# Inverse roots of two layer norms: pow on GpSimd, or Sqrt on ScalarE and a reciprocal on VectorE

## The reference

```python
def _layernorm(x, axis=-1, eps=1e-05):
    m = jnp.mean(x, axis=axis, keepdims=True)
    v = jnp.var(x, axis=axis, keepdims=True)
    return (x - m) / jnp.sqrt(v + eps)
...
x = x + jnp.tanh(g_xattn[0]) * _L0_xattn_ref(ctx_1024, _layernorm(x, axis=-1), ...)
x = x + jnp.tanh(g_ffn[0]) * _L0_ffn_ref(_layernorm(x, axis=-1), ...)
x = x + jnp.tanh(g_xattn[1]) * _L1_xattn_ref(_layernorm(x, axis=-1), ctx_1024, ...)
x = x + jnp.tanh(g_ffn[1]) * _L1_ffn_ref(_layernorm(x, axis=-1), ...)
```

## Time and profile before

| | |
|---|---|
| three runs | 1621.97, 1613.87, 1620.56 us; median 1620.56 |
| the profiled execution | 1621.97 us, of which the span of the profile is 1620.1 |
| busy share of the span | PE 91%, DVE 70%, ACT 60%, POOL 33% |
| mean granted clock of PE | 0.96 |
| attention block starts at | 873 us of the span |
| FFN block starts at | 1427 us of the span |

### The profile page before, as it was taken

The page is one execution under the profiler, slowest core; times in us unless marked ns, Lnnn a source line. Parts: engine busy times, 40 slices in busy tenths (PEclk is TensorE's granted clock), DMA queues, the critical chain, the costliest instruction groups (busy, mean ns, idle before and its releaser), DMA issues. The chain is left out here.

```text
span 1620.1 us, 21635 instructions
## 1 busy us (share of the span) xinstructions
PE 1466.9 (91%) x6308; PEld 640.0 (40%) x6309; DVE 1139.5 (70%) x1679; ACT 976.4 (60%) x1528; POOL 531.1 (33%) x342
## 2 busy tenths in 40 slices
PE   5678988889979899999999788899999999999899
PEld 2334434434434344444444343332333333244344
DVE  7989999999986222222223857789999999548975
ACT  3999999999933001111111542477878878868764
POOL 0679788688950710000003655605000000000000
PEclk7899989989989999999999899899999999999999
DMA  5202102002572565357524625354232332120344
GB/s 180 70 21 57 48 21 72 20 23 70 181 246 101 194 135 196 129 193 262 201 91 142 214 93 160 113 189 118 72 88 76 81 83 76 53 104 1 70 110 120
DMA packets 133478, 181.30 MB, mean 112 GB/s; under 512 B 46451, under 2 KB 80627, under 8 KB 132387
## 3 DMA queue, kind: packets, MB, share of 16 engines
q1 hardware_dynamic: 111878, 132.48, 27.7%
q0 software_dynamic: 6624, 23.14, 4.7%
q10 hardware_dynamic: 14912, 24.89, 4.6%
HBM read 109.29 MB, written 54.92 MB: 101 GB/s over the span
## 5 line engine op out<-in xcount | busy, mean ns | idle before, releaser
L265 POOL TENSOR_TENSOR m_hs<-m_hs,m_C 128x1024 f32<-128x1024 f32 x128 | 302.3, 2379 | 76.1 <-DVE m_hs L476 75.5
L1811 DVE TENSOR_REDUCE a_mx<-a_s 128x2 f32<-128x1024 f32 x256 | 303.2, 1218 | 33.1 <-PE a_s L1925 29.7
L476 DVE TENSOR_TENSOR_SCAN m_hs<-m_dA,m_d 128x512 f32<-128x512 f32 x256 | 293.7, 1200 | 9.4 <-PE m_d L622 8.5
L622 PE MATMUL m_d<-ident_sb,m_dBuT 128*128 128x128 f32 x1024 | 161.3, 289 | 30.8 <-DVE m_hs L476 23.2
L622 PEld LDWEIGHTS m_d<-ident_sb,m_dBuT 128*128 128x128 f32 x1024 | 115.7, 145 | 159.4 <-DVE m_hs L476 86.0
L371 ACT ACTIVATE m_dA<-m_dt,m_negA 128x512 f32<-128x512 f32 x256 | 168.1, 710 | 6.3 <-DVE m_hs L476 4.4
L1249 PE MATMUL e_gu<-e_w,e_xgT 128*128 x376 | 169.2, 592 | 0.0
L349 ACT ACTIVATE m_dBuT<-m_dtuT,m_BT 128x512 f32<-128x512 f32 x241 | 157.7, 710 | 0.1
L1925 PE MATMUL a_s<-ring_sb 96*128 96x512 bf16 x512 | 150.2, 383 | 4.5 <-DVE a_mx L1811 3.1
L917 ACT ACTIVATE e_sg<-e_gu 128x256 f32<-128x256 f32 x47 | 18.0, 384 | 224.6 <-PE e_gu L1249 224.6
L637 PE MATMUL m_y<-m_hs,m_fold 128*64 128x512 f32 x512 | 143.0, 639 | 0.4 <-POOL m_hs L265 0.4
(11 more groups left out here) (335 smaller groups left out, 2449.2 us busy)
## 6 DMA issues: line engine op xcount, KB each, us to landing
e_w<-in_ex_gu SPq DMA_DIRECT2D x16, 1024.0 KB, 6.2
ring_sb<-qk_dram SPq DMA_DIRECT2D x64, 192.0 KB, 3.1
xg_dram<-zeros_sb SPq DMA_DIRECT2D x2, 6016.0 KB, 28.3
e_xg<-xg_dram ACTq DMA_DIRECT2D x47, 256.0 KB, 2.7
yg_dram<-attn_sb ACTq DMA_DIRECT2D x47, 256.0 KB, 2.0
m_C<-c_dram SPq DMA_DIRECT2D x64, 128.0 KB, 2.9
m_dt<-m_dt SPq DMA_DIRECT2D x64, 128.0 KB, 2.3
e_w<-in_ex_dn SPq DMA_DIRECT2D x16, 512.0 KB, 7.5
```

The lines of the kernel that those rows point to most:

```text
L265: pool.tensor_tensor(hs[:, J % RH], hs[:, J % RH], C2[:, N % RC].unsqueeze(1).broadcast_to([P, 2, L]), ALU.mult).then_inc(s_hc, 1)
L476: dve.tensor_tensor_scan(hs[:, J % RH, h], dA[:, j % RA], pd[j % RD][:], 0.0, ALU.mult, ALU.add)\
L622: last = pe.transpose(pd[j % RD][:, t * P:(t + 1) * P], dBuT[:, N % 2, t, g], ident[:])
L1811: dve.tensor_reduce(mx[:, r % 2, h * TB + 2 * c:h * TB + 2 * c + 2], psc[c][:], AX.X, ALU.max)\
```

## The change

In both blocks the pow on POOL goes, with the `power` column it reads and its wait. ACT gets a function `std(b)`, a Sqrt in place on the four columns, and DVE's `inverse(b)` gets a reciprocal ahead of the `nmr` instruction. The new Sqrts stand on ACT after value 9 (batch 0), after value 15 (1), after `normalise(1)` (2) and after `normalise(2)` (3); in the FFN block ahead of each `normalise(b)` for batches 0 to 2, and that of batch 3 right after `normalise(2)`. `normalise(b)` waits as before for `inverse(b)`, whose semaphore now counts two steps for each batch.

```diff
@@ attention, gpsimd
-            def inverse_root(b):
-                cols = slice(b * TB, (b + 1) * TB)
-                pool.wait_ge(s_st, 2 * b + 2)
-                pool.tensor_tensor(rstd[:, cols], rstd[:, cols], power[:], ALU.pow).then_inc(s_rs, 1)
-
-            pool.memset(power[:], -0.5).then_inc(s_pw, 1)
-            pool.wait_ge(s_pw, 1)
...
-                if t in (8, 12):
-                    inverse_root(t // TB - 2)
-            inverse_root(2)
-            inverse_root(3)
@@ attention, scalar
+            def std(b):
+                act.wait_ge(s_st, 2 * b + 2)
+                cols = slice(b * TB, (b + 1) * TB)
+                act.activation(rstd[:, cols], rstd[:, cols], ACT.Sqrt).then_inc(s_sd, 1)
...
             def normalise(b):
-                act.wait_ge(s_inv, b + 1)
+                act.wait_ge(s_inv, 2 * b + 2)
...
             for t in range(10):
                 copy_v(t)
+            std(0)
             copy_v(10)
             copy_v(11)
             normalise(0)
             for t in range(12, NT):
                 copy_v(t)
+            std(1)
             normalise(1)
+            std(2)
             normalise(2)
+            std(3)
             act.preload_act_table_set("natural_log_exp_and_others")
@@ attention, vector
             def inverse(b):
                 cols = slice(b * TB, (b + 1) * TB)
-                dve.wait_ge(s_rs, b + 1)
+                dve.wait_ge(s_sd, b + 1)
+                dve.reciprocal(rstd[:, cols], rstd[:, cols]).then_inc(s_inv, 1)
+                dve.wait_ge(s_inv, 2 * b + 1)
                 dve.scalar_tensor_tensor(nmr[:, cols], mv[:, cols, 0], -1.0, rstd[:, cols], ALU.mult, ALU.mult)\
                     .then_inc(s_inv, 1)
@@ FFN, gpsimd
-            pool.memset(power[:], -0.5).then_inc(s_c, 1)
-            pool.wait_ge(s_c, 4)
-            for b in range(NT // TB):
-                cols = slice(b * TB, (b + 1) * TB)
-                pool.wait_ge(s_ln, SEQ * (b + 1))
-                pool.tensor_tensor(rstd[:, cols], rstd[:, cols], power[:], ALU.pow).then_inc(s_rs, 1)
@@ FFN, scalar
+            def std(b):
+                cols = slice(b * TB, (b + 1) * TB)
+                act.wait_ge(s_ln, SEQ * (b + 1))
+                act.activation(rstd[:, cols], rstd[:, cols], ACT.Sqrt).then_inc(s_lsd, 1)
+
             def normalise(b):
-                act.wait_ge(s_q, 2)
-                act.wait_ge(s_inv, b + 1)
+                act.wait_ge(s_inv, 2 * b + 2)
...
             round_weight(0)
+            std(0)
             normalise(0)
             square(1)
+            std(1)
             normalise(1)
             weight_std(1)
             round_weight(1)
             copy_x(0)
+            std(2)
             normalise(2)
+            std(3)
@@ FFN, vector
             def inverse(b):
                 cols = slice(b * TB, (b + 1) * TB)
-                dve.wait_ge(s_rs, b + 1)
+                dve.wait_ge(s_lsd, b + 1)
+                dve.reciprocal(rstd[:, cols], rstd[:, cols]).then_inc(s_inv, 1)
+                dve.wait_ge(s_inv, 2 * b + 1)
                 dve.scalar_tensor_tensor(nmr[:, cols], mv[:, cols, 0], -1.0, rstd[:, cols], ALU.mult, ALU.mult)\
                     .then_inc(s_inv, 1)
```

More of the change, by code:

```diff
@@ L1395, in attention @@
         rstd = sb("rstd", [P, NT])
-        power = sb("power", [P, TB])
         nmr = sb("nmr", [P, NT])
@@ L1436, in attention @@
         s_st = sem("ln_steps")
-        s_pw = sem("power_set")
-        s_rs = sem("ln_inverse_roots")
+        s_sd = sem("ln_std")
         s_inv = sem("ln_ready")
@@ L2102, in attention_out_and_ffn @@
         s_ln = sem("ln_steps")
-        s_rs = sem("ln_inverse_roots")
+        s_lsd = sem("ln_std")
         s_inv = sem("ln_columns")
```

## The result

| | before | after |
|---|---|---|
| median of 16 runs each | 1620.07 us | 1629.78 us |
| lowest and highest | 1610.91, 1622.68 | 1619.82, 1638.85 |
| the profiled execution (its span) | 1621.97 (1620.1) | 1638.13 (1636.0) |
| start of the attention block | 873.2 | 872.7 |
| `rotate(0)` after that start | 54.8 | 71.1 |

The ratio of after to before is 1.0062, with a 95% interval of 1.0045 to 1.0080: about 10 us lost where 1.2 were to be won. The profiled execution of after is among its longest (16.2 us above that of before), and its 16 runs lie 19 us apart, those of before 12.

What follows compares the result with a forecast made beforehand. PE is busy nine tenths of the span; POOL's pow was taken as on the path at the attention block's start. Attention -1.4 and FFN +0.2 gave -1.2 us, from the 1620.56 median to 1619.4; range 1612.7 to 1623.5.

Steps and rivals of the forecast that it cites:

- Batch 0: Attention block start: one table load, no DVE wait for the first Sqrt, nmr(0) done at 895.1, 4.0 us sooner.
- Batch 1, where the stall goes,: Attention start: DVE waits 4.7 us for Sqrt(1), behind ACT's copies of value tiles 12 to 15; 1.5 us stay won.
- POOL without pow, its gathers at one pace: Sign expected in the attention block's profile after: POOL issues its gathers evenly, with no pow among them.
- Batches 2 and 3: Attention block: no DVE wait before the third reciprocal; rotate(0), normalise(3) and PE's transposes come 1.4 us sooner.
- nothing arrives: Rival, chance 0.20: the 1.4 us are lost between 937 and 1040; only the FFN's +0.2 stands, giving 1620.8 us.
- A shift is carried to the end: Assumption: a shift of the point where rotate(0) starts in the attention block reaches the kernel's end.
- FFN, +0.2: FFN block: the reciprocal in inverse(3) adds 0.2 us on the chain; the first Gelu's later load stays hidden.
- Slower: Sqrt(1) stuck behind the copies: Rival, chance 0.10: attention block, PE projects at 1.2 GHz, DVE gets nmr(1) 6.2 us later; kernel takes 1627.0 us.
- More through the clock: Rival, chance 0.20: attention block, shorter PE idle time keeps its clock at 2.4 GHz; gain 3.3 us, 1617.3 us.
- The scatter: Whole kernel: before's three runs lie 8.1 us apart, more than every term; slower by over 0.5% got 0.03.

Runs made afterwards that it cites:

- the first experiment: Kernel after, with an unused pow of 128x4 put back on POOL behind the gathers of tiles 8 and 12: 1619.34 us, 0.9989 of before.
- the thirteenth: Kernel after, with four writes of 128x384 on POOL behind the gathers of tiles 8 and 12: 1619.18 us, 0.9997 of before.
- the eleventh: Kernel after, with unused pows behind the gathers of tiles 8 and 12 and behind every eighth scatter: 1615.10 us, 0.9949 of before.
- the fourteenth: Kernel after, with an unused pow of one column on POOL behind the gathers of tiles 8 and 12: 1621.58 us, 1.0012 of before.
- the seventh: Kernel before, with an unused pow on POOL behind every eighth of the experts' block's 32 scatters: 1617.09 us, 0.9970 of before.
- the fifteenth run: Kernel after, with an unused pow on POOL behind the gathers of tile 8 only: 1621.80 us, 1.0023 of before.
- the fifth experiment: Kernel after, with POOL issuing tile t's gathers only once those of tile t-2 have landed, no pow: 1623.43 us, 1.0015 of before.
- 3: Kernel after, with Sqrt(1) moved ahead of the copies of value tiles 12 to 15 on ACT: 1631.53 us, 1.0065 of before.
- 4: Kernel before, with the attention part of the change alone, FFN block as before: 1626.87 us, 1.0040 of before.
- the sixth experiment: Kernel after, with a one-column write on POOL after each tile's gathers: 1636.11 us, 1.0092 of before.
- 8: Kernel after, with one-column writes on POOL after each tile's gathers and each scatter of the experts' block: 1638.36 us, 1.0097 of before.
- 2: Kernel after, with only the old roots' waits put back on POOL behind the gathers of tiles 8 and 12: 1635.43 us, 1.0080 of before.

## Why the prediction was wrong, step by step

*Batch 0* was right to a tenth: no idle time of DVE ahead of its first reciprocal, nmr(0) done 21.85 us after the block's start in place of 25.90, that is 4.05 sooner (predicted 4.0), one load of 1.28 us and no more. The load starts 0.02 us after the end of the copy before it, and the Sqrt 0.01 us after the load's end (892.46 + 1.28 = 893.74). The drain of 1.38 us that the Trainium skill (ScalarE: Activation LUTs, What ACT_TABLE_LOAD costs) adds to a switch isn't seen.

*Batch 1, where the stall goes,* is the step that failed. The wait was named, in its place and with its releaser, and it is there. But its size came from a stretch of 13.8 us between nmr(0) and the last copy, read in the trace of before, where two pows interrupted POOL's gathers, and carried over into a kernel in which they don't. In after the stretch is 925.94 + 0.60 - 894.51 = 32.0 us. That is 18.2 more, and ACT's four remote waits in it sum to 17.9; in each of them PE's matmuls were done before ACT came free. With the pows put back and nothing else the wait was 5.7 us, against 4.7 predicted: the stretch holds where its condition does. The prediction took "POOL without pow, its gathers at one pace" for harmless, and priced POOL's relief at nothing or a gain.

*Batches 2 and 3.* No wait before the third reciprocal, as predicted. Whether `rotate(0)` comes 1.4 us sooner with the train broken isn't settled: it stands at 54.9 in the first experiment, 54.1 in the thirteenth, 53.9 in the eleventh and 51.6 in the fourteenth, against 54.8 before, a gain of -0.1 to 3.2 us in single profiles. The first experiment's ratio, 0.9989 (0.9974 to 1.0004), allows both the forecast's gain of 1.2 us and none, so the rival "nothing arrives" isn't excluded for the change without its side effect.

*A shift is carried to the end:* right, if not to the tenth. `rotate(0)` moved by 16.3 us and the FFN block by 17.6.

*FFN, +0.2:* right. DVE's timeline of after, up to its first maximum of the hidden tiles:

```profile
1516.17 0.17 DVE L2309 RECIPROCAL f_rstd<-f_rstd 128x4 f32<-128x4 f32 x1
1516.38 0.16 DVE L2311 SCALAR_TENSOR_TENSOR f_nmr<-f_mv,f_rstd 128x4 f32<-128x4 f32 x1
1516.46 2.34 DVE L2383 TENSOR_REDUCE f_am<-attn_sb 128x1 f32<-128x1024 f32 x2
```

The same in the kernel with the attention part alone, whose FFN block is that of before:

```profile
1512.25 0.15 DVE L2308 SCALAR_TENSOR_TENSOR f_nmr<-f_mv,f_rstd 128x4 f32<-128x4 f32 x1
1512.33 2.34 DVE L2380 TENSOR_REDUCE f_am<-attn_sb 128x1 f32<-128x1024 f32 x2
```

The block's first table load is at 1444.08 and 1440.16, so the maxima come 72.38 and 72.17 us after it: 0.21 later. The Gelu's load is 0.59 later (68.12 against 67.53), for 0.6 predicted, and hidden. Against the trace of before itself these numbers say nothing: there PE had a granted clock of 0.65 (between 1.2 and 2.4 GHz) in the block's first 3 us, where it had 1.00 in the run of the FFN part alone, its first eight matmuls for DVE took 5.11 us in place of 3.70, and the whole block lies 1.4 us later for that.

*The rivals.* "Slower: Sqrt(1) stuck behind the copies" had the place and the sign, and by luck nearly the price (1627.0; measured 1629.8), but not the mechanism: PE's signals, counted late. PE at the lower of its two clocks (1.2 and 2.4 GHz) came only behind that: the eight matmuls from 905.05 took 4.95 us and the eight from 919.63, after 9.63 us of idle time, 6.27, where sixteen took 7.69, 3.5 us more together. Its chance of 0.10 rested on the clock alone. "More through the clock": PE stood still for 1.39 us before the transposes in place of 5.92, and its clock stayed at 1.00 from 896 to 900, as that rival had it; what it won was lost in the late signals. In the profile of the fourteenth experiment, where hardly a signal is late, the clock stays at 1.00 from 893 to 905, the sixteen matmuls take 7.03 us in place of 7.69, and `rotate(0)` is 3.2 us sooner, about what the rival had (1.4 and 2.1 together). Its median of 1621.6 doesn't show that gain.

```profile
896.00:900.00 4.00, 1.97 (x12) 1.00 1.01 364
900.00:904.00 4.00, 0.00 (x0) 0.62 1.06 360
904.00:914.00 10.00, 5.86 (x12) 0.81 0.73 220
914.00:919.00 5.00, 0.00 (x0) 0.56 0.58 161
919.00:928.00 9.00, 6.33 (x9) 0.68 0.06 20
```

(The columns are the stretch, its length, PE's busy time, its granted clock, the share of the DMA engines and GB/s.)

*The scatter.* I had put 3 in 100 on slower by over 0.5%, from the spread of before's three runs. The range failed for its cause, not for the spread.

**What stays open.** Why a semaphore that PE's matmul raises is counted late while POOL issues indirect DMAs. The runs show when it happens (only PE's signals were seen late, from 22 to 25 us into the first train of gathers on, and 4 and 14 us into the second one in experiments 7 and 15) and what takes most of it away, not the mechanism. Whether it is the gathers under way or POOL's issuing as such wasn't told apart: the fifth experiment changed both. Two figures of the traces bear on it, and point different ways. In after the gathers don't pile up: from 903 us on the last packet of each ends 3.3 to 3.5 us after its issue began, while signals are late by up to 10.7 us. But the signals of value tiles 12 and 13 are counted at 918.96 and 919.02, 3.1 us after POOL had issued the last gather and 0.8 after its last packet; in experiments 3, 4, 6 and 8 it is 3.0 to 3.6 and 0.6 to 1.3 us. And each wait and each "rotate(0)" is of one profiled execution.

## What to carry to other kernels

An instruction on a helper engine can have a use that no wait shows: the gaps it makes in that engine's own DMA issue. Before you take the last interruption out of a train of indirect DMAs, look in the trace for waits with the releaser `remote` while another such train runs unbroken; if they are there, they may well appear in yours. In this kernel a pause of about 1 us after every eighth scatter, and after gathers 18 and 26 of 32, cost less than it saved; after every fourth scatter it won no more. Look at the trace again afterwards: signals can be late between two pauses too. And a stretch read from the trace of before holds only while all engines that share it go on as they did: check for each engine what it stops doing, not only what it no longer has to wait for.

## What the runs showed of the hardware

- With POOL issuing an indirect DMA about every 1.3 us without a pause, semaphores raised by PE's matmuls were counted 4.8 to 9.1 us after the matmul's end in after, those of the value tiles 9 to 11; in the sixth experiment up to 13.1, and in the block of the experts 18.0. In the same stretch of after ACT's reached PE within 0.1 us.
- The lateness begins 24.5 us into the train of gathers in after (22 to 23 in experiments 2, 3, 4, 6 and 8), some 20 us into the train of scatters, 14 us into the second train of gathers in the fifteenth run and some 4 us into that of the seventh. Pauses of 0.6 to 1.9 us by a pow or by writes, or waits of up to 2.6 us for a landing, took most or all of it away; a write of 0.12 us between two gathers and a wait already met did nothing.
- A pow of 128x4 on POOL takes 1.00 to 1.59 us (median 1.07), one of 128x1 0.60 and 0.96, four writes of 128x384 together 1.9.
- The kernel before has room left by this alone: four pows among its scatters, 0.9970 (0.9954 to 0.9986).
